# A product-key FFN on Trainium2: a quarter of each one-hot block goes to ScalarE, and the next step's similarities go in front of the row matmuls

## The reference, cut to what matters

```python
q = jnp.einsum('bnd,de->bne', x, w_q)            # 2 * 8 heads * 128, then batch norm over all tokens
sim = jnp.einsum('pbnhd,hkpd->pbnhk', q, keys)   # 2 halves, 8 heads, 32 keys
sx, ix = jax.lax.top_k(sim[0], TOPK)             # TOPK = 8
sy, iy = jax.lax.top_k(sim[1], TOPK)
all_scores = (sx[..., :, None] + sy[..., None, :]).reshape(b, n, H, TOPK * TOPK)
all_indices = (ix[..., :, None] * NUM_KEYS + iy[..., None, :]).reshape(b, n, H, TOPK * TOPK)
scores, pk = jax.lax.top_k(all_scores, TOPK)
indices = jnp.take_along_axis(all_indices, pk, axis=-1)
wd = down_embed[indices]                         # 1024 experts
wu = up_embed[indices]
h = jnp.einsum('bnd,bnhkd->bnhk', x, wd)
h = gelu_new(h)
h = jax.nn.softmax(scores, axis=-1) * h
out = jnp.einsum('bnhk,bnhkd->bnd', h, wu)
```

## Time and profile before

| | before |
|---|---|
| median of 3 runs | 1323.63 us |
| lowest and highest | 1322.28, 1325.7 us |
| the profiled execution | 1320.99 us |
| its span | 1319.3 us |
| TensorE busy | 1168.6 us (89%) |
| VectorE busy | 1133.0 us (86%) |
| ScalarE busy | 890.4 us (67%) |
| POOL busy | 621.4 us (47%) |

### The profile page before, as it was taken

How to read it: one execution, slowest core, us unless ns; L and a number is a source line. 1 busy time by engine, 2 the same in 40 slices (tenths; PEclk the granted TensorE clock), 3 DMA queues, 4 the chain that set the end, 5 groups by cost and what they waited for, 6 DMA issues and landing times. The chain is left out here.

```text
span 1319.3 us, 32707 instructions
## 1 busy us (share of the span) xinstructions
PE 1168.6 (89%) x12762; PEld 909.4 (69%) x12762; DVE 1133.0 (86%) x2847; ACT 890.4 (67%) x1260; POOL 621.4 (47%) x520
## 2 busy tenths in 40 slices
PE   6778999999999999999999999999997839877778
PEld 4655676767777777777777767677776727767678
DVE  6547998999989899998999999898986688999984
ACT  5559788888888888888889878888884332212121
POOL 3215757577575667757567675667330310000000
PEclk9679999999999999999999999999999766556666
DMA  8107999999999999999999999999998300000000
GB/s 173 24 24 148 184 197 194 195 192 194 191 188 199 202 192 198 197 198 196 191 197 190 196 190 195 185 188 185 180 187 135 105 0 2 5 5 6 5 5 6
DMA packets 665392, 186.25 MB, mean 141 GB/s; under 512 B 653938, under 2 KB 662294, under 8 KB 664854
## 3 DMA queue, kind: packets, MB, share of 16 engines
q1 hardware_dynamic: 665238, 184.16, 81.1%
HBM read 19.97 MB, written 0.82 MB: 16 GB/s over the span
## 5 line engine op out<-in xcount | busy, mean ns | idle before, releaser
L1169 PE MATMUL ps<-pT,xa_hi 128*128 128x128 f16 x2288 | 381.2, 217 | 26.3 <-DMA pT<-p 25.9
L978 ACT ACTIVATE e<-ps,bias 128x1444 f32<-128x1444 f32 (+1 forms) x208 | 305.4, 1468 | 126.5 <-DVE bias L1051 125.2
L1165 PE MATMUL ps<-pT,xa_hi 128*128 128x128 f16 x2288 | 383.1, 217 | 6.3 <-ACT uT L1001 5.6
L1166 PE MATMUL ps<-pT,xa_lo 128*128 128x128 f16 x2288 | 383.1, 217 | 0.0
L1049 DVE TENSOR_REDUCE nmax<-ps 128x1 f32<-128x1444 f32 (+1 forms) x208 | 344.0, 1654 | 33.3 <-PE ps L1149 32.8
L1061 DVE TENSOR_TENSOR p<-e,p 128x1408 f16<-128x1408 f32 (+3 forms) x288 | 303.5, 1095 | 31.5 <-ACT p L986 30.4
L986 ACT ACTIVATE p<-e 128x1408 f16<-128x1408 f32 (+1 forms) x208 | 288.2, 1386 | 13.3
L934 POOL TENSOR_TENSOR p<-e,p 128x1408 f16<-128x1408 f32 (+1 forms) x128 | 196.6, 1557 | 181.6 <-ACT p L986 181.6
L1169 PEld LDWEIGHTS ps<-pT,xa_hi 128*128 128x128 f16 x2288 | 222.0, 98 | 33.9 <-DMA pT<-p 33.6
L1165 PEld LDWEIGHTS ps<-pT,xa_hi 128*128 128x128 f16 x2288 | 222.2, 98 | 30.0 <-issue 15.1
L1147 PE MATMUL ps<-xT_hi,q_hi 128*128 128x512 f16 (+1 forms) x624 | 229.0, 367 | 5.0 <-POOL q_lo L923 3.2
(11 more groups left out here) (235 smaller groups left out, 1938.8 us busy)
## 6 DMA issues: line engine op xcount, KB each, us to landing
raw<-in_ctx SPq DMA_DIRECT2D x16, 704.0 KB
pT<-p SPq DMA_TRANSPOSE x416, 4.2
f_wq<-in_L_ffn_w_q SPq DMA_DIRECT2D x1, 1024.0 KB, 5.0
f_wqt<-in_ffn_wq_t SPq DMA_DIRECT2D x2, 512.0 KB, 6.7
raw<-in_ctx SPq DMA_DIRECT2D x48, 18.0 KB
x_tok<-in_x SPq DMA_DIRECT2D x4, 200.0 KB
out_x<-ost SPq DMA_DIRECT2D x6, 128.0 KB, 2.0
wk_t<-in_wk_t SPq DMA_DIRECT2D x1, 512.0 KB, 10.0
```

What stands on the lines that cost most here:

```text
L978: act.activation(e32[t % E_BUF][rows, :], score_banks(t)[rows, 0:T], ACT.Exp, bias=bias[rows, t % N_BUF:t % N_BUF + 1]).then_inc(e_done, 1)
L1165: pe.matmul(out, hi, ph, start=n == 0, stop=False)
L1166: pe.matmul(out, lo, ph, start=False, stop=False)
L1169: pe.matmul(out, hi, pl, start=False, stop=False)
```

## The change

Three things change in the steps.

TensorE does `sims(i+1)` right behind `hidden(i,0)`, ahead of the rows of step i-1. ScalarE copies them out ahead of the exponentials instead of behind them.

VectorE makes the one-hot blocks only of the first `S_DVE` = 96 of the 128 tokens. ScalarE makes the other 32, in full steps: for each token an `Abs` of r minus `iota_r` (32 instructions of 128 elements, with the token's r as the bias), which is zero in one place and at least 1 elsewhere, and then one `Relu` of 1 minus that over all 4096 elements. A copy of the last 32 columns of r in float (`r_late`) serves as the bias. The fourth group of rows waits for ScalarE (`oneh_act`). A new constant `iota_r` is written by POOL in the setup.

VectorE takes the first `EARLY` = 6 of the 32 (in the last step, of the 16) maxima of step i+1 already in step i, between weigh 3 and `oneh`, and waits for `simb` there.

```diff
+EARLY = 6
+S_DVE = 3 * P // 4
...
             pool.wait_ge(fc_done, 6)
+            pool.tensor_copy(iota_r[:, :], iota_f[:, :])
...
                 picks(i)
+                if i + 1 < NSTEP:
+                    sims_out(i + 1)
                 act.wait_ge(dsc_done, i + 1)
                 act.activation(esc[0:w, 0:nh, :, :], dsc[0:w, 0:nh, :, :], ACT.Exp).then_inc(esc_done, 1)
-                if i + 1 < NSTEP:
-                    sims_out(i + 1)
                 act.wait_ge(selT_ps, i + 1)
...
                 act.activation(cT[0:j, 0:w], ps[0:j, 4, P:P + w], ACT.Identity, bias=off8[0:j, 0:1]).then_inc(selT_done, 1)
+                if w == P:
+                    act.activation(r_late[0:j, :], ps[0:j, 4, S_DVE:P], ACT.Copy).then_inc(far_done, 1)
                 act.activation(w_hi[0:j, 0:w], ps[0:j, 4, 2 * P:2 * P + w], ACT.Copy).then_inc(selT_done, 1)
+                if w == P:
+                    act.wait_ge(far_done, 2 * i + 1)
+                    act.wait_ge(narrow_done, 1)
+                    if i:
+                        act.wait_ge(g_ps, group_number(i, 0))
+                    for t in range(S_DVE, P):
+                        ins = act.activation(oneh[0:j, :, t], iota_r[0:j, :], ACT.Abs, bias=r_late[0:j, t - S_DVE:t - S_DVE + 1], scale=-1.0)
+                    ins.then_inc(far_done, 1)
+                    act.wait_ge(far_done, 2 * i + 2)
+                    act.activation(oneh[0:j, :, S_DVE:P], oneh[0:j, :, S_DVE:P], ACT.Relu, bias=1.0, scale=-1.0).then_inc(oneh_act, 1)
...
-                        for n in range(NB):
+                        for n in range(EARLY if hf == 0 else 0, NB):
                             ins = dve.max(top[0:w, hf, n, :], simb[0:w, hf, n, :])
...
+                if i + 1 < NSTEP:
+                    dve.wait_ge(sim_done, i + 1)
+                    for n in range(EARLY):
+                        dve.max(top[0:step_shape(i + 1)[1], 0, n, :], simb[0:step_shape(i + 1)[1], 0, n, :])
+
...
-                dve.tensor_tensor(out=oneh[0:j, :, 0:w], in0=iota_w[0:j, :, 0:w],
-                                  in1=rT[0:j, 0:w].rearrange("p (a s) -> p a s", a=1).to_broadcast([j, P, w]), op=ALU.is_equal)
+                we = min(w, S_DVE)
+                dve.tensor_tensor(out=oneh[0:j, :, 0:we], in0=iota_w[0:j, :, 0:we],
+                                  in1=rT[0:j, 0:we].rearrange("p (a s) -> p a s", a=1).to_broadcast([j, P, we]), op=ALU.is_equal)
...
+                if n == S_DVE // QP:
+                    pe.wait_ge(oneh_act, i + 1)
...
             for i in range(NSTEP):
                 hidden(i, 0)
+                if i + 1 < NSTEP:
+                    sims(i + 1)
...
-                if i + 1 < NSTEP:
-                    sims(i + 1)
                 turned(i)
```

More of the change, by code:

```diff
@@ L1216, in ffn @@
         off8 = sb("off8", [P, 1])
+        iota_r, r_late = sb("iota_r", [P, P], F16), sb("r_late", [P, P - S_DVE])
         iota_w = sb("iota_w", [P, P, P], F16)
@@ L1272, in ffn @@
         wide_idx, soft_done = sem("wide_idx"), sem("soft_done")
+        far_done, oneh_act = sem("ffar_done"), sem("foneh_act")
         block = ctx.enter_context(nc.Block())
```

## The result

| | before | after |
|---|---|---|
| median | 1322.95 us | 1347.78 us |
| lowest and highest | 1320.02, 1325.7 us | 1346.32, 1351.19 us |
| the profiled execution, its span | 1320.99, 1319.3 us | 1351.19, 1349.2 us |

The ratio is 1.0197, with a 95% interval from 1.0175 to 1.0218. The change makes the kernel 2% slower. The forecast was 1308.7, faster. What came is rival A, near its far end (1353).

The account below looks back on a forecast made before the run. Bound: the wait through rows, similarities, simb and rT before oneh, with VectorE having little air. Periods of 34.57 us, less a 3.2 us later step 0, gain 14.9 us, giving 1308.7 us; range 1303 to 1317.

Parts of the forecast that it names:

- rival A: ScalarE's strided Abs pass is too slow: 1313.7 at 0.39 us each, 1353 at 0.594; chances 0.09 and 0.06.
- ScalarE's part: 32 Abs at 0.297 us make 9.6 us, Relu 3.7; gel ends at T+40.7, so nobody waits, cost nothing.
- the cover of 2.2 us: ScalarE finishes gel at T+40.7, 2.2 us before TensorE's hidden(i+1,1) needs it at T+42.9.
- Who waits, and from where on: hidden(i+1,1) on TensorE needs gel; beyond 0.364 us per Abs, each 0.01 us costs 1.9 in six steps.
- Similarities first: Moved ahead of the rows; oneh starts at T+24.4, gaining 5.3 us over five steps.
- T+24.4: Start of oneh, counted from T, the end of mv_lo, where one step's row matmuls are released.
- The one-hot of 96: VectorE's oneh loses 4096 elements, saving 2.13 us in each of six steps; T lies 10.17 after its start.
- TensorE's window: Between two row groups, transposes, add_experts, hidden and similarities end at T+33.1 to 34.2, fitting before T+34.57 by 0.4 to 1.5.
- Step 0: Similarities stand between the halves of hidden; esc comes 3.2 us late, oneh starts at 1078.4 instead of 1075.21.
- A's far part: ScalarE's Abs take beyond 0.44 us each; from 0.442 the whole gain is gone, 1353 at 0.594; chance 0.06.
- near part of A: ScalarE's Abs take between 0.364 and 0.44 us each; 1313.7 at 0.39; chance 0.09.

Follow-up runs that it names:

- e1: Changed kernel with ScalarE's 32 blocks in their own tile, written contiguously, and TensorE loading them from there; 1305.46 us, ratio 0.9864.
- e2: Changed kernel without ScalarE's part: VectorE makes all 128 blocks, similarities first and early maxima stay; 1317.9 us, ratio 0.9963.
- e3: Changed kernel with 16 tokens for ScalarE instead of 32, same strided writes; 1310.6 us, ratio 0.9913.
- e5: e1 with the similarities at their old place and no early maxima, so ScalarE's part alone; 1302.28 us, ratio 0.9863.
- e10: e5, but the fourth row group loads blocks 64 to 95 of VectorE's tile with the 264-byte stride; 1309.29 us, ratio 0.9909.
- e8b: e1 with 64 contiguous Abs instead of 32, half of them into a spare tile; 1345.98 us, ratio 1.0182.
- e7: e1 with step 0 in the old order on TensorE and ScalarE; 1302.74 us, ratio 0.9858.
- e4: Kernel before plus a first set of write measurements behind its last step: Copy and Abs at several distances, VectorE copies; 1352.85 us, measurements included.
- e9: Kernel before plus a second set of measurements behind its last step: float writes, pairs and fours of two-byte elements; 1340.66 us, measurements included.

## Why the prediction was wrong, step by step

**ScalarE's part: the term that failed.** "I take 0.297, for the same operands and source" priced the Abs by what it reads and what operands it has, and took the cover of 2.2 us from that. The pass took 18.9 us instead of 9.6, and so the wait for gel, which was put at nothing, was 6.5 to 6.8 us in five steps and 6.0 in the last. The nearest row was near in everything but the place of the result. Its second failure is the argument against rival A, that TensorE reads with this same stride at 65 ns per 128 elements. That is a read, and of another engine; it says nothing of two-byte writes. The 113 ns that it set beside them come from a row of ScalarE whose 4096 results are neighbours, and so hold for no other stride: 132 apart, 128 elements cost 560. And the 65 ns were themselves the price of the stride: contiguous blocks take 33.

The Trainium skill's rule for A (SBUF — State Buffer, "Door 1: The DMA port swizzle"), a penalty for each new line of 16 bytes, came out for this write: single two-byte elements 8 or more apart cost 0.51 to 0.57 us for 128, closer ones less. The measurements differ where each element or pair opens a line of its own and yet costs little: float elements 8 and 32 apart cost 0.23 and 0.21, hardly more than contiguous ones, and 256 elements in pairs 0.35.

**Who waits, and from where on: right.** The pass was said to decide from 0.364 us per Abs, by way of gel and hidden(i+1,1), and TensorE's wait for gel between the rows was named as the sign of being wrong. It came at that place. With a pass 9.3 us longer and 2.2 us of cover the account gives 1308.7 + 6 x 7.1 = 1351; measured 1347.8. The cover was 2.7 to 2.9 us: in the step of e1 that is shown, gel ended at 1197.46 and hidden began at 1200.34. The 9.45 us by which the pass is longer than in e1, less this cover, are the 6.6 us or so that TensorE waited.

**Similarities first: right in kind.** oneh at T+24.4 was forecast; in e1 it starts at T+24.2 (1216.02, T being 1181.65 + 10.17). e2 has 36.6 for 36.7, e1 34.4 for 34.57, e3 35.5 for 35.7. What the forecast did not see is that the move is needed only as long as TensorE loads all blocks with a stride (e5, e10).

**The one-hot of 96: right.** 6.56 us, as worked out.

**TensorE's window: right, at its edge.** 0.4 to 1.5 us of air were forecast. In the steps with full similarities behind the transposes it was 0.7, 0.9 and 1.0 in the changed kernel, and 1.5, 1.7 and 0.2 in e1. In the last of these the granted clock rose 6.0 us after the transposes began (at 1186.41, from 1180.43), in the one before 2.8 us after, so the forecast's low end was a little too high.

**Step 0: too dear in four traces of six,** and it goes with when the clock rises. The table of 1 us stretches of the changed kernel has the clock still at 1.2 GHz 5 us after the similarities began at 1064.5, and rising in the last of these:

```profile
1069.00:1070.00 1.00, 1.00 (x3) 0.78 (x3) 1.00 (x12) 0.00 (x0) 0.00 (x0) 0.50 0.00 0
1070.00:1071.00 1.00, 1.00 (x5) 0.87 (x4) 0.92 (x6) 0.00 (x0) 0.00 (x0) 0.85 0.00 0
```

In e8b, too, it rose 5.8 us after their start (1059.9). In e2 it rose 3.6 us after it (1057.5, rising at 1061.1), and hidden ran at 2.4 GHz as a whole. Why it rose sooner in some executions is open.

**The chances: wrong.** A's far part had 0.06. The prediction said itself that no row showed such a write; a term without a row, with a factor of two between its ends and 2.2 us of cover in front of 15 us of gain, deserved more than that. The range ended at 1317, which the prediction's own slope (1.9 us for each 0.01) puts at 0.407 us per Abs, so it didn't even hold the whole near part of A.

**The best version of these** is ScalarE's part in a tile of its own with everything else as before (e5, 1302.3, ratio 0.9863), or the same with all moves but those of step 0 (e7, 1302.7). Both beat both kernels, and by their ratios neither can be told apart from the other or from e1 (0.9864). With a short pass and contiguous blocks no gain of the moves is shown.

## What to carry to other kernels

Price an instruction by where it writes, too: a row with the same engine, size and operands is no neighbour if its result is contiguous and the new one is scattered in single two-byte elements. When an idle engine takes work over, look for what it had to do next for someone else; here ScalarE had 28 us of idle time, the pass as forecast took 13 of them, and yet only 2.7 to 2.9 us more were free, since gel stood behind. And a layout kept for one engine (tokens innermost, as VectorE writes them here) may cost the reader twice the time: a part of the work that changes engines is free to change its layout with it.

## What was not expected of the hardware

- ScalarE, 128 elements, written by one instruction after another: 0.20 us for two-byte elements 2 apart, 0.28 for 4 apart, 0.51 to 0.57 for 8 to 132 apart (e4, e9; 0.575 in the changed kernel); pairs of two bytes 132 apart cost 1.4 ns an element; float 0.21 to 0.23 at 8 and 32 apart. Of reading, 128 two-byte elements 128 apart, written as contiguous float: 0.30.
- VectorE's copy of 128 two-byte elements came every 0.10 us contiguous, and with the elements 132 apart every 0.30 in the last five of eight (behind the last step of e4).
- A row matmul, with a weight load of 128 x 128 two-byte elements ahead of it, follows the last by 65 ns if the columns of a row of weights lie 264 bytes apart, and by 33 if they are neighbours (e5, granted clock 0.5).
